# First graph layer: column sums taken from a column of ones, products issued before the verdict on the block

## What is computed

```
x = x + gnn0(layernorm(x), adj)      # two layers of the following
x = x + ffn0(layernorm(x))           # eight experts, routed by argmax
x = x + adj @ (layernorm(x) * W)
x = x + ffn1(layernorm(x))           # routed by segment

def layer(h, M):                     # THRESH 1e-6, EPS 1e-8
    A = M / (sum(M, axis=0) + EPS)
    mask = A > THRESH
    W = where(mask, A, 0)
    T = h @ W_in + b_in
    agg = where(any(mask, axis=0), (W.T @ T) / (sum(W, axis=0) + EPS), T)
    out = agg @ W_out + b_out + h @ W_self + b_self
    return normalise_rows(out) * gamma + beta
```

## Time and profile before

| | us |
|---|---|
| median of three runs (1068.97 to 1069.34) | 1069.16 |
| the profiled execution | 1073.89 |
| its span, first to last instruction | 1072.2 |

### The profile page before, as it was taken

How to read it: one execution, slowest core, us unless ns; L and a number is a source line. 1 busy time by engine, 2 the same in 40 slices (tenths; PEclk the granted TensorE clock), 3 DMA queues, 4 the chain that set the end, 5 groups by cost and what they waited for, 6 DMA issues and landing times.

```text
span 1072.2 us, 12873 instructions
## 1 busy us (share of the span) xinstructions
PE 1020.4 (95%) x3642; PEld 536.4 (50%) x3642; DVE 563.1 (53%) x1539; ACT 320.8 (30%) x627; POOL 225.9 (21%) x217
## 2 busy tenths in 40 slices
PE   4989999999999999999999899959999999999997
PEld 1435555555455544444444377723454554454544
DVE  6688888888821234434334444553543534435365
ACT  3654764664521100000000053404223123132231
POOL 4011331332322012122121224443110110100101
PEclk9999999999999999999999999979999999999999
DMA  9969855655200488888872663236664655555400
GB/s 360 408 237 316 285 203 227 235 225 209 117 1 1 157 303 310 321 297 314 302 300 100 261 216 92 82 85 235 236 227 176 236 187 213 195 204 193 157 1 20
DMA packets 45357, 220.98 MB, mean 206 GB/s; under 512 B 6626, under 2 KB 27940, under 8 KB 33634
## 3 DMA queue, kind: packets, MB, share of 16 engines
q1 hardware_dynamic: 42146, 215.60, 54.2%
q0 software_dynamic: 2864, 4.39, 1.2%
q10 hardware_dynamic: 272, 0.13, 0.0%
HBM read 210.68 MB, written 11.62 MB: 207 GB/s over the span
## 4 chain that ended last, share of the span: by engine, by line
PE 78%; DVE 12%; DVEq 3%; issue 3%; DMA 2%; ACT 2%; POOL 1%; SPq 0%; another core or an unknown queue 0%; POOLq 0%; ACTq 0%
PE PA L1545 31%; PE PA L1750 20%; DVE R L928 7%; PE O L1727 3%; PE O L1793 3%; PE O L1588 3%; PE PA L1508 2%; DMA ring<-in_adj_cols 2%; PE T L1802 1%; PE SR L1793 1%; PE T L1813 1%; PE SM L1793 1%; PE PA L1717 1%; PE O L1772 1%; ACT U L667 1%
## 5 line engine op out<-in xcount | busy, mean ns | idle before, releaser
L1750 PE MATMUL PA<-ring,S 128*128 128x512 f32 x512 | 233.4, 596 | 2.2 <-ACT S L682 2.2
L1545 PE MATMUL PA<-ring,S 128*128 128x512 f32 x512 | 229.8, 597 | 0.1
L1545 PE MATMUL PA<-ring,U 128*128 128x512 f32 x512 | 226.2, 595 | 0.0
L1545 PEld LDWEIGHTS PA<-ring,U 128*128 128x128 f32 x512 | 94.9, 190 | 107.2 <-issue 107.1
L1545 PEld LDWEIGHTS PA<-ring,S 128*128 128x128 f32 x512 | 96.0, 191 | 103.5 <-issue 101.5
L928 DVE TENSOR_TENSOR R<-R,ring 128x1024 f32<-128x1024 f32 x98 | 138.9, 1418 | 7.1 <-issue 1.8
L1750 PEld LDWEIGHTS PA<-ring,S 128*128 128x128 f32 x512 | 92.1, 190 | 100.6 <-issue 96.1
L576 ACT ACTIVATE work<-ring 128x2048 int8<-128x2048 f32 x64 | 122.3, 1910 | 42.0 <-DMA ring<-in_adj_cols 38.6
L1414 DVE TENSOR_TENSOR U<-ring,work 128x512 f32<-128x512 f32 x112 | 84.2, 759 | 85.1 <-PE SR L1793 42.1
L868 POOL DMA_DIRECT2D out_x<-work x7 | 5.9, 844 | 233.1 <-DVE work L1485 233.1
L827 POOL DMA_INDIRECT disp_d<-work x32 | 32.0, 999 | 96.5 <-DVE work L1260 89.1
(11 more groups left out here) (241 smaller groups left out, 1157.4 us busy)
## 6 DMA issues: line engine op xcount, KB each, us to landing
ring<-in_adj_cols SPq DMA_DIRECT2D x56, 2048.0 KB, 7.6
ring<-in_adjT_cols SPq DMA_DIRECT2D x32, 2048.0 KB, 7.3
work<-in_w SPq DMA_DIRECT2D x16, 256.0 KB
ring<-in_Wr SPq DMA_DIRECT2D x1, 4096.0 KB, 13.6
ring<-in_Wr SPq DMA_DIRECT2D x2, 2048.0 KB, 18.1
disp_d<-U SPq DMA_DIRECT2D x4, 650.0 KB, 10.3
work<-disp_d SPq DMA_DIRECT2D x8, 325.0 KB
S<-in_x SPq DMA_DIRECT2D x4, 512.0 KB, 5.9
```

Source lines behind the costliest of these rows:

```text
L1545: mm = nc.tensor.matmul(out_T[:, :], X[:, t * D:(t + 1) * D], ring[slot][t // HT][:, (t % HT) * BW:(t % HT + 1) * BW], start=n == 0, stop= ...
L1750: mm = nc.tensor.matmul(PA[slot][:, :], S[:, t * D:(t + 1) * D], ring[1][t // HT][:, (t % HT) * BW:(t % HT + 1) * BW], start=t == 0, stop= ...
```

## The change

1. **Ones column.** `normalise_x` writes 127 of the 128 columns of S; the last is set to 1. Row 127 of every product is then the column sum. As a normalised row adds up to 0, its last value is minus the sum of the others: the weights take this in, W_in with its last row subtracted from all (`t_in1d`), W_self by a product with the matrix `minus`.
2. **Order on TensorE.** Products of block k start without a verdict. `column_sums(k)` takes row 127 out of the aggregate (by `sel`) after it is complete, inside step k+1 behind two tiles; `sum_verdict(k)` follows two tiles later, `out_rows(k)` at tile 9, `turn_z(k)` at 20, `layer2_products(k)` at 23. The self part is a piece of its own (`self_rows(k)`, at 29 of step k).
3. **VectorE** loses all adds over the ring. It runs the tail of a block in one piece: `aggregate` (copy from PSUM), `verdict`, `mask_if_needed`, `empty_rows` (from GpSimd), `scales`, `bias_rows` (from ScalarE and GpSimd), `out_tiles`, `moments`, `layer2_inputs`, `self_rows(k+1)`.
4. **The branch body** (still skipped) now also multiplies the masked block anew on VectorE (`masked_products`).
5. **Ring.** A slot is refilled only after the verdict on the block in it, all four quarters at once.
6. **Start.** x comes in five parts laid out by partition, between the quarters of the first block; twelve small matmuls on `ident` come ahead of the first products. The weights come as one large array and five small. `FIRST_PIECES` puts `turn_h` at tile 28 and `weight_products` at tile 30.
7. The blocks go in the order 7,6,5,4,3,2,0,1 (before 7 to 0), and layer two takes the rows of the last quarter in their plain order.

```diff
+XPARTS = ((0, 4), (4, 8), (8, 16), (16, 24), (24, 32))
...
+            load_x(0)
+            load_x(1)
+            load_first(0, s_first)
+            load_x(2)
+            load_first(1, s_ring[slot_of(0)][0])
+            load_quarter(sp, adjc, blk(0), slot_of(0), 1)
+            load_x(3)
+            load_quarter(sp, adjc, blk(0), slot_of(0), 2)
+            load_x(4)
+            load_quarter(sp, adjc, blk(0), slot_of(0), 3)
             for dst, name in WEIGHTS:
...
             def refill(k):
                 for q in range(4):
-                    if q < 3:
-                        sp.wait_ge(s_quart, (k - 2) * 3 + q + 1)
-                    else:
-                        sp.wait_ge(s_agg, k - 1)
-                    alone(sp)
-                    load_quarter(sp, adjc, blk(k), k % 2, q)
+                    load_quarter(sp, adjc, blk(k), slot_of(k), q)
                     empty_buffers(k, q)
...
+            for k in range(NB):
+                store_thr(k)
+                if k + 2 < NB:
+                    refill(k + 2)
...
-            for k in range(NB):
+            for k in range(1, NB):
                 evac_hT(k)
...
+                empty_cols(k - 1)
+                check(k, 0)
+                check(k, 1)
+                normalise(k - 1)
+                relu_h1(k - 1)
+                check(k, 2)
+                check(k, 3)
...
             for k in range(NB):
-                empty_rows(k)
-                if k > 0:
-                    moments(k - 1)
-                else:
-                    pool.wait_ge(s_wready, 1)
-                add_bias(k)
-                if k > 0:
-                    own_T2(k - 1)
+                moments(k)
+                own_T2(k)
...
-            for c in range(XC):
+            for c, (lo, hi) in enumerate(XPARTS):
                 dve.wait_ge(s_xin[c], 16)
...
+                nc.vector.memset(tiles(S[:, lo * D:hi * D], hi - lo)[:, :, LAST:D], 1.0)
                 if c > 0:
                     normalise_x(c - 1)
             normalise_x(XC - 1)
...
+            def tail(k):
+                aggregate(k)
+                verdict(k)
+                mask_if_needed(k)
+                empty_rows(k)
+                scales(k)
+                if k == 0:
+                    self_rows(0)
+                dve.drain()
+                bias_rows(k)
+                out_tiles(k)
+                moments(k)
+                layer2_inputs(k)
+
+            fold_weights()
+            for k in range(1, NB):
+                tail(k - 1)
+                self_rows(k)
+            tail(NB - 1)
...
+            def column_sums(k):
+                pe.wait_ge(s_raw, k + 1)
+                for t in range(BT):
+                    last = nc.tensor.matmul(SM[:, t:t + 1], aT[:, t * P:(t + 1) * P], sel[:, 0:1], start=True, stop=True)
+                last.then_inc(s_sums, 1)
...
+                nc.tensor.matmul(SR[:, :], sel, aT, start=True, stop=True).then_inc(s_srow, 1)
...
+            L1_PIECES = ((2, turn_h, 0), (2, column_sums, 1), (4, sum_verdict, 1), (9, out_rows, 1), (20, turn_z, 1),
+                         (23, layer2_products, 1), (29, self_rows, 0))
+            FIRST_PIECES = ((28, turn_h, 0), (30, lambda k: weight_products(), 0))
```

More of the change, by code:

```diff
@@ L263, in build @@
         s_wts2 = sem("s_wts2")
-        s_xin = [sem(f"s_xin{c}") for c in range(4)]
+        s_xin = [sem(f"s_xin{c}") for c in range(XC)]
+        s_first = sem("s_first")
         s_ring = [[sem(f"s_ring{s}{q}") for q in range(4)] for s in range(2)]
@@ L1137, in _ @@
[L1137 to L1144 removed]
+                dve.wait_ge(s_hT, k + 1)
+                alone(dve)
+                nc.vector.tensor_tensor(U[:, cols_of(k)], U[:, cols_of(k)], hT[k % 2], ALU.mult)
@@ new lines, in self_rows @@
+            def self_rows(k):
+                pe.wait_ge(s_wready, 1)
+                pe.wait_ge(s_hT, k + 1)
+                for t in range(BT):
+                    if k > 0 and t % 2 == 0:
+                        pe.wait_ge(s_u2u, (k - 1) * 2 + t // 2 + 1)
+                    mm = nc.tensor.matmul(O[t // 2][:, t % 2 * DH:(t % 2 + 1) * DH], hT[k % 2][:, t * P:(t + 1) * P], W_s1[:, :], start=True, stop=True)
+                    if t % 2 == 1:
+                        mm.then_inc(s_self, 1)
@@ L1564, in turn_h, with out_rows @@
+            def out_rows(k):
+                pe.wait_ge(s_aT, k + 1)
+                for t in range(BT):
+                    if t % 2 == 0:
+                        pe.wait_ge(s_zpre, k * 2 + t // 2 + 1)
+                    nc.tensor.matmul(O[t // 2][:, t % 2 * DH:(t % 2 + 1) * DH], aT[:, t * P:(t + 1) * P], W_io[:, :], start=True, stop=True).then_inc(s_o1, 1)
             def turn_h(k):
+                if k >= 1:
+                    pe.wait_ge(s_hT, k)
                 if k >= 2:
@@ L1612, in step @@
-            def step(k):
-                pe.wait_ge(s_clean, k + 1)
-                if k >= 2:
-                    pe.wait_ge(s_aT, k - 1)
+            L1_PIECES = ((2, turn_h, 0), (2, column_sums, 1), (4, sum_verdict, 1), (9, out_rows, 1), (20, turn_z, 1),
+                         (23, layer2_products, 1), (29, self_rows, 0))
+            FIRST_PIECES = ((28, turn_h, 0), (30, lambda k: weight_products(), 0))
+            def step(k, pieces):
                 done = 0
-                for n, piece in L1_PIECES:
-                    products(S, k % 2, done, n, s_quart)
-                    piece(k)
+                for n, piece, back in pieces:
+                    if n > done:
+                        products1(k, done, n)
+                    piece(k - back)
@@ L1620, in step @@
                     done = n
-                products(S, k % 2, done, NT, s_quart).then_inc(s_agg, 1)
-            first_block_tiles()
-            raw_sums(0)
-            pe.wait_ge(s_hn, XC)
-            keep_warm(1, S[:, 0:BW], PA[0])
-            sum_verdict(0)
-            keep_warm(2, S[:, 0:BW], PA[0])
-            for k in range(NB):
-                step(k)
+                products1(k, done, NT).then_inc(s_agg, 1)
+            pe.wait_ge(s_const, 1)
+            for _ in range(WARM):
+                nc.tensor.matmul(PA[1][:, 0:P], ident[:, :], ident[:, :], start=True, stop=True)
@@ L1633, in tail_a @@
+            step(0, FIRST_PIECES)
+            for k in range(1, NB):
+                step(k, L1_PIECES if k > 1 else L1_PIECES[:3] + ((6, self_rows, 1),) + L1_PIECES[3:])
             def tail_a(k):
```

421 lines of the change are left out of this document (177 added, 244 removed).

## The result

| | before | after |
|---|---|---|
| median of four runs, us (lowest to highest) | 1069.16 (1068.97 to 1069.34) | 1052.73 (1051.33 to 1054.12) |
| profiled execution: time, span, us | 1073.89, 1072.2 | 1051.33, 1049.6 |
| start of step 1, us | 82.45 | 49.19 (forecast 49.5) |
| from there to the end of `step2(0)`, us | 301.1 | 315.1 (forecast 301.9) |
| VectorE busy, us | 563.1 | 424.1 |

The ratio is 0.9846 (95% interval 0.9833 to 0.9858): 16.4 us less where 32.2 were forecast, and outside the range of 1030 to 1050. The start came as worked out. What is missing was lost in the stretch behind it, from step 1 to `step2(0)`.

The account below looks back on a forecast made before the run. TensorE was taken to bound the steps, while the first 41.32 us ran no product of the layer. Gains and losses of 33.0 - 0.75 - 0.05 = 32.2 took the median from 1069.16 to 1037.0 us, range 1030 to 1050.

Parts of the forecast that it names:

- Part 1: Start of the layer up to step 1: step 1 begins at 49.5 us instead of 82.45, a gain of 33.0.
- the clock falls and comes back: TensorE after its 6.6 us pause ahead of tile 8: 5.7 us at half speed, charged at 2.85 us.
- 24.6 us of products: Products of block 0 that TensorE still had to run once the third quarter was there, 32 tiles.
- price of a tile: TensorE's products: 0.86 us for each tile, 27.5 us for 32.
- Part 2: Seven further steps of layer one: 37.8 us each, 266.3 in all against 265.55, a loss of 0.75 us.
- From it to the first instruction behind the branch are 1.53 us: VectorE's chain in each step: time from the flag's copy past the skipped branch, read from the old trace.
- the margins of 1.0 and 0.6: Microseconds by which VectorE's results precede TensorE's request in a step, at `out_rows` (`s_aT`) and at `turn_z`.
- Rival (a): VectorE's jump over the longer branch body costs 2 us more in each of eight blocks: 11 us, 1048; chance 19%.
- Part 3: `step2(0)`, the stretch behind the steps: 35.6 us against 35.55, so no change.
- Part 4: Ring refills waiting for the verdict, 7.5 us into a step: quarters still land in time, cost nothing.
- The sum: All parts together: 33.0 - 0.75 - 0.05 = 32.2 us gained, median 1037.0.

Follow-up runs that it names:

- e3_keep_clock: e6_compact with six warming products added in TensorE's pause ahead of tile 8; 1035.93 us.
- e7_norm_first: e6_compact with the third and fourth part of x normalised ahead of the wait for the next part; 1032.84 us.
- e6_compact: The changed kernel with the masked products as one loop over 128 features instead of four over 32, a jump of 107 instructions; 1037.90 us.
- b1_before_again: The kernel before, unchanged, for a second profiled execution; that took 1069.25 us.
- e8_mid_body: e6_compact with 73 one-element writes added in the branch body, a jump of 180 instructions; 1048.86 us.
- e10_shift20: e8_mid_body with 20 one-element writes on VectorE ahead of its first statistics; 1057.01 us.
- e12_taken: e6_compact with the branch always taken in block 0; 7822.83 us, a single run.

## Why the prediction was wrong

- **Part 1, the new start: right.** Tile 8 at 22.80 (22.8), step 1 at 49.19 (49.5). That the clock falls and comes back was right; its price was 2.2 and not 2.85 (e3_keep_clock), because part of the half speed fell into the pause itself. (The 24.6 us of products left when the third quarter is there should read 27.5, by the prediction's own price of a tile; no sum uses it.) The pause was avoidable at once (e7_norm_first).
- **Part 2, the steps: the failed step.** "From it to the first instruction behind the branch are 1.53 us" was carried over from before, where the jump passes 56 instructions, to one that passes 244 (134 rows of the listing that was counted). The trace shows a wait for an instruction fetch there in six of eight blocks, for which the sum had nothing. With a short body the same sum holds: in e6_compact 37.76 us a step (37.8), 266.4 for the seven (266.3), and 302.2 to the end of `step2(0)` (301.9). With the long one six jumps are 2.2 to 2.5 us longer, the margins of 1.0 and 0.6, which were about right, are used up, and the stretch takes 315.1: 13.2 of the missing 15.8 us.
- **Rival (a) was the mechanism**, at 19%, with 2 us more in eight blocks and 1048; it was some 2.3 more in six, and each cost 2.1 and not 1.4 (39.81 against 37.76 us: TensorE's waits of 1.2 and 0.36, and busy time of 38.25 instead of 37.76 around them). That its 1048 lies near the measured time is in part luck: too many blocks at too low a price. The mechanism that the Trainium skill's section "Instruction fetch mechanics" names is the one found; taken at its size, two blocks of 256 with the next one at hand, it would have had a jump of 244 not wait. The rival should have weighed more, because the traces of before already had a mark of it: behind the same jump L1036 starts after two different idle times. VectorE's timeline of the second execution (b1_before_again), blocks 3, 4 and 6:

```profile
147.13 0.18 DVE L1036 RECIPROCAL small<-small 128x4 f32<-128x4 f32 x1 [1.01 <-issue]
...
185.75 0.18 DVE L1036 RECIPROCAL small<-small 128x4 f32<-128x4 f32 x1 [1.38 <-issue]
...
262.23 0.18 DVE L1036 RECIPROCAL small<-small 128x4 f32<-128x4 f32 x1 [1.00 <-issue]
```

  In both executions the drain stands 0.21 us behind the branch in blocks 2, 3, 6 and 7 and 0.49 to 0.57 in the others. A jump of one length with two prices, in the same blocks each time, says that its place among fetched blocks counts; the earlier trace rows showed one of them only.
- **Part 3, `step2(0)`: right but for its jump.** 37.87 against 35.6, with the long jump that ends at 336.10. In e6_compact, with a short one, the window is the forecast's to 0.2:

```profile
88.42:126.18 37.76, 37.76 (x121) 20.73 (x120) 12.49 (x44) 20.81 (x24) 3.77 (x5) 1.00 0.76 293
314.98:350.78 35.80, 35.80 (x112) 19.03 (x110) 11.44 (x44) 4.21 (x7) 4.28 (x9) 1.00 0.37 136
```

- **Part 4, the ring: right.** No wait for a quarter in the steps.
- **The sum.** The forecast gain is 32.2. Off it go 13.2 for the six long jumps, 1.8 for the longer tail, and 1.4 because the profiled execution of after lies that far below its median; 0.3 come on top at the start, and 0.4 because the first part is that much longer in before's second execution. That makes 16.5, against a measured 16.4. Without the long jumps, e6_compact gains 31.5, close to the forecast of 32.2.

## What to carry to other kernels

Code in a branch that is never taken can have a price: count the instructions that the jump passes, on the engine's own stream, and keep them few (here jumps over 56 and 107 never waited, over 244 six times of eight), or give the engine that waits behind it 2.5 us of margin. Where one and the same jump shows two prices in a trace, places decide, and a few instructions added anywhere ahead can then move a time by about one per cent. And look at a loop that waits for its next input before it finishes the last one.

## What was new about the hardware

- In the kernels with the change a jump on VectorE takes, from the branch to the instruction behind it, 0.2 us where no fetch is near it (two of eight in e6_compact), 0.5 to 0.6 where one begins 1.1 to 1.4 us behind the branch, and 2.7 to 3.1 where one begins ahead of the landing, at 180, 244 and 444 instructions alike. The long one has an extra 8 KB fetch, 2.4 to 2.7 us ahead of the next. In idle time to the next working instruction these are 1.2, 1.6 to 1.9 and 3.8 to 4.4 us.
- A jump that lands two instructions ahead of an edge is short and still costs 3.7 us of idle time, two instructions later (block 3 of e8_mid_body, block 7 of e10_shift20).
- Twenty one-element writes ahead of the layer cost 8.2 us (1048.86 to 1057.01), ninety gave 9.3 back (1039.59).
- The turn of a hardware loop on VectorE with one instruction and a drain has 0.64 us without work beside the 0.75 of the instruction (e12_taken).
